# Setup of a fused four-layer kernel: weight loads issued earlier, batch 0 packed ahead of its period, conversions moved to earlier slots

## What is computed

```python
x = L0(x)   # x -> gelu(x down) -> an expert chosen by the batch's id -> up, + x, layer norm
x = L1(x)   # scale and shift from a timestep; attention, 16 heads of 16, with bias and mask; FF of 1024
x = L2(x)   # one of three small MLPs, chosen by the batch's id, + x, layer norm
x = L3(x)   # finite differences of products with five 256x256 grids, x + dt * sum, relu

emb = silu(sin_emb(timestep)) @ W_ada + b_ada      # in L1
q, k, v = x @ Wq + bq, x @ Wk + bk, x @ Wv + bv
probs = softmax(where(mask, -inf, q k' / 4 + attention_bias))
x = x + (probs v) @ Wo + bo
x = x + gelu2(ln(x) * g2 @ W1 + b1) @ W2 + b2
```

## Time and profile before

| | us |
|---|---|
| median of 3 runs | 895.62 (894.95 to 899.71) |
| profiled execution, its own time | 897.77 |
| profiled execution, its span | 896.0 |
| TensorE busy in the span | 817.8 (91%) |
| DVE busy | 739.6 (83%) |
| ACT busy | 623.2 (70%) |

### The profile page before, as it was taken

One profiled execution on the slowest core, in us unless ns is written; L12 is line 12 of the kernel. 1 busy time (PEld: TensorE's weight loads), 2 busy tenths in 40 slices (PEclk: granted clock), 3 DMA queues, 4 the chain that ended last, 5 costly groups with the idle time before them and its releaser, 6 DMA issues.

```text
span 896.0 us, 18592 instructions
## 1 busy us (share of the span) xinstructions
PE 817.8 (91%) x5968; PEld 698.8 (78%) x5968; DVE 739.6 (83%) x2474; ACT 623.2 (70%) x1284; POOL 163.8 (18%) x160
## 2 busy tenths in 40 slices
PE   5576869899999999999999999999999999998692
PEld 2355658788988888888888888888888888787581
DVE  5452787898998989898989899898989898969555
ACT  3153758687878787887878787878788787777230
POOL 3010101222030302122222213030212212201200
PEclk9677989999999999999999999999999999999986
DMA  6356978577585868676676857595758678581110
GB/s 173 117 129 159 206 173 195 129 173 178 133 192 149 190 153 173 156 187 164 157 185 168 189 134 179 151 193 154 183 156 177 162 155 175 138 200 43 53 36 12
DMA packets 147593, 137.33 MB, mean 153 GB/s; under 512 B 19282, under 2 KB 144787, under 8 KB 147492
## 3 DMA queue, kind: packets, MB, share of 16 engines
q1 hardware_dynamic: 147172, 135.80, 63.8%
q10 hardware_dynamic: 320, 0.26, 0.1%
HBM read 98.23 MB, written 4.23 MB: 114 GB/s over the span
## 4 chain that ended last, share of the span: by engine, by line
PE 82%; DVE 9%; issue 3%; SPq 2%; DMA 2%; ACT 1%; POOL 0%; POOLq 0%; DVEq 0%; ACTq 0%
PE back_bank L1109 12%; PE turn_bank L1065 11%; PE score_bank L1184 6%; PE context_bank L1119 6%; PE score_bank L1185 6%; PE front_bank L1103 5%; PE back_bank L1103 5%; PE attend_bank L1103 5%; PE front_bank L1136 3%; PE back_bank L1089 3%; PE front_bank L1290 3%; PE back_bank L1080 3%; PE attend_bank L1089 3%; PE attend_bank L1050 2%; PE front_bank L1338 2%
## 5 line engine op out<-in xcount | busy, mean ns | idle before, releaser
L548 ACT ACTIVATE sc<-sc,negmax 128x256 f32<-128x256 f32 x512 | 231.2, 504 | 20.6 <-DVE negmax L905 20.1
L905 DVE CUSTOM_DVE_ANT_0 sc<-score_bank,side 128x256 f32<-128x256 f32 x512 | 195.3, 419 | 40.4 <-PE score_bank L1185 33.0
L526 ACT ACTIVATE pt<-turn_bank 128x512 f32<-128x512 f32 x176 | 105.9, 602 | 133.3 <-PE turn_bank L1065 112.3
L1065 PE MATMUL turn_bank<-ident,sc 128*128 128x128 f32 x1024 | 158.4, 278 | 1.4 <-ACT sc L548 1.4
L1065 PEld LDWEIGHTS turn_bank<-ident,sc 128*128 128x128 f32 x1024 | 124.3, 142 | 32.6 <-issue 14.1
L1184 PE MATMUL score_bank<-ks,qs 128*128 128x256 f32 x512 | 124.0, 324 | 8.5 <-DVE negmax L905 6.2
L1109 PE MATMUL back_bank<-w,ffT 128*128 128x256 f32 x512 | 118.0, 379 | 0.0
L1109 PEld LDWEIGHTS back_bank<-w,ffT 128*128 128x128 f32 x512 | 97.0, 190 | 12.6
L1185 PE MATMUL score_bank<-mask_neg,ident_r 128*128 128x512 f32 x256 | 102.8, 402 | 0.0
L468 POOL TENSOR_TENSOR rstd<-var,half_neg 128x2 f32<-128x2 f32 x64 | 50.0, 781 | 286.9 <-DVE var L830 285.3
L1184 PEld LDWEIGHTS score_bank<-ks,qs 128*128 128x128 f32 x512 | 79.6, 195 | 16.6 <-issue 7.9
(11 more groups left out here) (216 smaller groups left out, 1978.1 us busy)
## 6 DMA issues: line engine op xcount, KB each, us to landing
side<-in_side SPq DMA_DIRECT2D x128, 512.0 KB, 5.4
qs<-qh SPq DMA_DIRECT2D x128, 64.0 KB, 4.3
qs<-ql SPq DMA_DIRECT2D x128, 64.0 KB, 4.6
wb<-in_wb SPq DMA_DIRECT2D x16, 512.0 KB, 7.2
ks<-kh SPq DMA_DIRECT2D x126, 64.0 KB, 4.1
ks<-kl SPq DMA_DIRECT2D x126, 64.0 KB, 4.5
xN<-in_x SPq DMA_DIRECT2D x16, 256.0 KB, 4.8
wc<-in_wc SPq DMA_DIRECT2D x16, 256.0 KB, 3.1
```

The source lines that it names most:

```text
L526: e.activation(pt[:, h % NP2, :, :], two(tbank[h % 2]), ACT.Copy).then_inc(copied[h % 4], 1)
L548: i = e.activation(sc[:, h % NS, q, :], sc[:, h % NS, q, :], ACT.Exp, bias=negmax[:, q, h:h + 1], scale=-1.0)
L905: i = e.tensor_tensor_reduce(sc[:, s % NS, q, :], two(sbank[s % 2])[:, q, :], side[:, (H * X.i + s) % NSIDE, q, :], -1.0, 3.4e38, ALU.add, ...
L1065: i = e.transpose(tbank[h % 2][:, k * S + q * P:k * S + q * P + P], sc[:, h % NS, q, k * P:k * P + P], ident[:, :])
```

## The change

The load of `w1` takes the place of that of `w2` behind the first inputs; that of `w_ada` goes to a buffer of its own (in `sc`), since `w1` now lies in `ffT`. The rest of the weights, 12 transfers of 3.8 MB in all by their sizes in the code, is issued at turn -1, slot 1. Both halves of batch 0 are packed in turn -1, and period 0 has no `stack(X, B, 1, ..)`. ACT's Gelu table is loaded at the start, and Sin stands behind the first Gelu. The conversions move as in the list.

```diff
             load(ld_bo, (bo[:, :], d["bo"].partition_broadcast(P)), (wo[:, :, :], blocks(d["wo"])))
-            load(ld_bo, (w2[:, :, :], blocks(d["w2"])))
+            load(ld_w1, (w1_raw, blocks(d["w1"])))
...
-            later = {
-                (0, 1): lambda: load(ld_w1, (w1_raw, blocks(d["w1"]))),
-                (0, 3): lambda: load(ld_grid, (t_a[:, :, :], tall(d["grid_B"][0]))),
...
-            }
+            def load_rest():
+                load(ld_bo, (w2[:, :, :], blocks(d["w2"])))
+                load(ld_grid, (t_a[:, :, :], tall(d["grid_B"][0])), (t_b[:, :, :], tall(d["grid_B"][1])), (t_c[:, :, :], tall(d["grid_B"][2])),
+                     (x2[:, :, :], tall(d["grid_A"][0])), (x3[:, :, :], tall(d["grid_A"][1])))
+                load(ld_late, (wa[:, :, :], blocks(d["wa"])), (t_u[:, :, :], blocks(d["d1T"])), (t_r2[:, :, :], blocks(d["d2T"])),
+                     (b2r[:, :], d["b2"].partition_broadcast(P)), (gamma3[:, :], d["gamma3"].partition_broadcast(P)),
+                     (beta3[:, :], d["beta3"].partition_broadcast(P)))
...
+                    if is_step(t, s, -1, 1):
+                        load_rest()
...
-                    if s in (0, 1, 2, 3) and X:
+                    if s in (0, 1, 2, 3) and X and t > 0:
                         stack(X, B, 1, (s,))
...
-                        for b in range(NBLK) if s == 8 else (2, 3):
-                            for u in range(2):
-                                (pack_q, pack_k)[s - 8](e, 0, b, u)
+                        for m, blocks_ in ((0, range(NBLK)),) if s == 8 else ((0, (1, 3)), (1, range(NBLK))):
+                            for b in blocks_:
+                                for u in range(2):
+                                    (pack_q, pack_k)[s - 8](e, m, b, u)
+                                    if m == 1:
+                                        pack_q(e, m, b, u)
...
+            e.wait_ge(pool_set, IDENT_SET)
+            e.activation(first_switch[:, :], ident[:, 0:1], ACT.Gelu)
...
-                    if t == 1 and s in (1, 2):
+                    if is_step(t, s, -1, 8):
                         e.wait_ge(ld_w1, 16)
-                        e.activation(w1[:, s - 1, :], w1_raw[:, s - 1, :], ACT.Copy, scale=g2c[:, s - 1:s]).then_inc(act_set, 1)
-                    if is_step(t, s, 1, 5):
+                        for k in range(KT):
+                            e.activation(w1[:, k, :], w1_raw[:, k, :], ACT.Copy, scale=g2c[:, k:k + 1]).then_inc(act_set, 1)
+                    if is_step(t, s, -1, 11):
                         e.wait_ge(ld_bo, 3 * 16)
                         e.activation(w2[:, :, :], w2[:, :, :], ACT.Copy, scale=0.5).then_inc(act_set, 1)
...
-                    for t0, s0, setup in ((-2, 5, set_high), (-2, 14, set_low_q), (-1, 2, set_first_ada), (-1, 3, set_rest), (-1, 4, set_ada_rows),
-                                          (-1, 7, set_value_bias), (-1, 11, set_output_bias), (1, 1, set_first_bias), (1, 2, set_scaled_grids),
-                                          (1, 3, set_first_low), (1, 4, set_more_grids), (1, 5, set_sum_grids), (1, 7, set_edges),
-                                          (2, 1, set_conditional), (2, 3, set_derivatives)):
+                    for t0, s0, setup in ((-2, 14, set_high_q), (-1, 2, set_first_ada), (-1, 3, set_low_q), (-1, 6, set_rest), (-1, 6, set_ada_rows),
+                                          (-1, 7, set_value_bias), (-1, 9, set_first_low), (-1, 10, set_output_bias), (-1, 11, set_scaled_grids),
+                                          (-1, 12, set_more_grids), (0, 1, set_sum_grids), (0, 3, set_conditional), (0, 5, set_edges),
+                                          (0, 7, set_derivatives), (0, 11, set_first_bias)):
```

More of the change, by code:

```diff
@@ L333, in _ @@
                  (upT[0:A, :], d["upT"]), (upT[ONE:ONE + 1, :], d["up_b"].rearrange("(a n) -> a n", a=1)))
-            load(ld_ada_w, (ffT[:, 0:4, :], blocks(d["w_ada"])))
+            load(ld_ada_w, (w_ada, blocks(d["w_ada"])))
             e.wait_ge(dve_set, IDS_SET)
@@ L594, in body @@
                         i.then_inc(ev["kh_ready"], 1)
+                        if t == -1:
+                            e.wait_ge(ev["kh_ready"], F.n)
+                            e.wait_ge(pool_set, KS_SET)
+                            for b in (0, 2):
+                                for u in range(2):
+                                    pack_k(e, 0, b, u)
                     if s == 9 and F:
@@ L717, in in_halves, with set_high @@
                 return w[:, k, m * P:m * P + P].rearrange("p (u d h) -> p u d h", d=DH, u=2)
[L719 to L724, removed]
+            def set_high(raw, high, low, scale):
+                for k, m, u in parts:
+                    i = e.tensor_scalar(in_halves(high, k, m)[:, u, :, :], by_half(raw, k, m)[:, u, :, :], scale, None, ALU.mult)
+                link(i)
             def set_low(raw, high, low, scale):
@@ L730, in set_low, with set_high_q @@
                 link(i)
-            def set_low_q():
-                set_low(*raws[0])
+            def set_high_q():
+                e.wait_ge(ld_proj, 3 * 16)
+                set_high(*raws[0])
             def set_first_ada():
@@ L738, in set_first_ada, with set_low_q, set_rest @@
                 link(e.tensor_copy(ada[:, 1, :], abank[:, D:2 * D]))
+            def set_low_q():
+                link(e.tensor_scalar(bq, bq, DH ** -0.5, None, ALU.mult))
+                set_low(*raws[0])
+                e.sem_inc(dve_set, 1)
+            def set_rest():
+                set_high(*raws[1])
+                link(e.tensor_copy(wv[:, :, :], th[:, 0, :, :]))
                 set_low(*raws[1])
[L741 to L744, removed]
+                link(e.tensor_tensor(wvl[:, :, :], th[:, 0, :, :], wv[:, :, :].bitcast(F32), ALU.subtract))
                 e.sem_inc(dve_set, 1)
@@ L1150, in body @@
                                 cond = x1late[:, k, 0:1].broadcast_to([P, P]) if rows == P else x1late[:, k, 0:NB]
-                                e.matmul(dst, cond, ffT[:, 2 * k:2 * k + 2, :], start=(k == 0), stop=False)
+                                e.matmul(dst, cond, w_ada[:, k, :], start=(k == 0), stop=False)
                             i = e.matmul(dst, ones_row[:, 0:rows], b_ada, start=False, stop=True)
```

39 lines of the change are left out of this document (12 added, 27 removed).

## The result

| | median us | all executions |
|---|---|---|
| before | 895.29 | 894.2 to 899.71 (4) |
| changed | 883.36 | 882.13 to 884.87 (4) |

The ratio is 0.9858, with a 95% interval of 0.982 to 0.9896: 11.9 us less. 881.5 was predicted, with a range of 876 to 889. The profiled execution took 884.87 us, its span 883.1, against 897.77 before. The total is thus near, but it is made of parts that were not all right, and these are what the profile shows.

The account below looks back on a forecast made before the run. TensorE was taken as the bound from 198 us on, so only its idle time before that could move. Terms -0.5 - 1.4 - 1.5 - 8.5 - 2.3 = -14.2 us led to 881.5 us, range 876 to 889.

Parts of the forecast that it names:

- Lead-in (A): Work up to the first scores of layer 0: about 0.5 us earlier, first scores at 50.4.
- w2 term of 1.1: In the lead-in, ACT's scaling of w2 between the two g delays the second g and first scores by 1.1 us.
- the prediction's own sign of 40: Store of ada_rows before the first packs: landing after 40 us would show the queue forecast wrong; 38.4 was expected.
- the second rival: Early weight loads run slower than 365 GB/s, at 217; first scores 6.2 us late, end 887.6; chance 0.17.
- Period 0 (B): Up to qh of batch 1: the 7.3 us pack wait goes, setup fills most of it; -1.4 us beside A.
- the sum 66.65 - 0.5 + 7.0 - 1.0 = 72.1: Forecast time of qh of batch 1: old end of q, lead-in gain, setup added, less short waits of DVE.
- Head 0 of batch 1 (C): Before the first scores of batch 1: one grid load less and a faster last pack landing; -1.5 us.
- the 0.6 of the grid load: Before head 0 of batch 1, SP has one grid load less to issue: 0.6 us gained.
- the predicted -3.4 to the first scores of batch 1: First scores of batch 1 come 3.4 us earlier in all.
- Period 1 (D): DVE's setup leaves period 1, where PE waited for DVE, and PE's clock rises: -8.5 us.
- Period 2 (E): set_conditional leaves period 2 and with it PE's idle time of 2.3 us: -2.3 us.
- The third rival: Setup in period 0 hides in waits for scores, qh near 67 to 68; another -4.5, end 877; chance 0.13.

Follow-up runs that it names:

- e7: Changed kernel plus 16 unused 512-column matmuls, 8 each in slots 3 and 5 of period 0: 880.93 us.
- e5: Changed kernel with ACT's scaling of w2 moved behind the second g of layer 0 instead of between the two: 882.03 us.
- the repetition: The changed kernel measured once more, unaltered, beside later runs on the same chip: 884.60 us.
- e1: Changed kernel with four setup steps (sum_grids, edges, conditional, derivatives) put back from period 0 to their old places in periods 1 and 2: 886.15 us.
- e3: Changed kernel's loads and packs, with all conversions it had moved out of periods 1 and 2 put back there: 890.41 us.
- e4: Changed kernel with conditional, derivatives, sum_grids and edges moved from period 0 into DVE's gaps of the lead-in: 876.29 us.
- e9: Changed kernel with sum_grids, conditional, edges and derivatives moved from slots 1, 3, 5 and 7 of period 0 to its slot 9: 877.00 us.
- e6: Changed kernel with the store of the conditional vectors issued by ACT instead of by SP behind the twelve loads: 883.01 us.
- e11: Changed kernel with the four setup steps in slot 9, w2 scaling behind the second g, store on ACT's queue, plus 16 unused matmuls: 874.67 us.

## Why the prediction was right, and where its terms were wrong

**Lead-in (A), predicted -0.5, measured +0.1.** The expert's matmul came 0.7 earlier and not 0.9 (12.56 after 13.29). The moves of DVE were as forecast: `n3l` 2.3 earlier (28.42), `ql` 2.1 earlier (33.36). Then the term lacked the clock: k's twelve matmuls took 2.89 us at 0.50 instead of 1.72 at full clock. That is no fixed price of the change, since k took 1.96 in e7 with the same lead-in, and the kernel before has one profile only. The w2 term of 1.1 was right (0.9 in e5).

**The packs.** The store landed at 39.4 and not 38.4, the packs began at 39.8, and the first half was issued by 47.5. Its last pack landed at 49.5, as written: 1.5 us ahead of the first scores here, 0.7 ahead in the repetition, where the store landed at 40.2, past the prediction's own sign of 40. In three profiles with a quicker lead-in the packs came last, and the first scores waited for them: 0.65 us in e7, 2.0 in e1, 2.4 in e3. Moving 3.8 MB ahead of a small transfer delayed it from 1.6 to 6.1, the behaviour the prediction reckoned with; the loads ran at 363 GB/s at 34 to 36 us, so the second rival's 217 GB/s did not come.

**Period 0 (B), predicted -1.4, measured +0.8 beside A.** The prediction set its forecast against 73.98, the second of the two writes of `qh`. Against the first, 73.61, its 72.1 is -1.5 in all and -1.0 beside A, and the 7.3 us of waiting are 7.0. The step that failed is the sum 66.65 - 0.5 + 7.0 - 1.0 = 72.1. It prices DVE's setup and leaves PE's own work at its old length. The price of the setup was nearly right: from the first scores to the start of q it is now 20.52 us instead of 14.03, +6.5 against the +6.0 of the sum, and +6.1 in the repetition. Then q takes 2.93 instead of 1.69: 1.2 us that the text had no term for. With the 0.6 of A that makes the 2.4 between 72.1 and 74.50. Ahead of q PE waited for DVE's steps (2.69, 2.53 and 2.00 us), with the clock at 0.50 from 52 to 62 us where it had been 0.66. That the steps are the reason for the half clock is likely but not shown, as e5, e1 and e3 say above.

**Head 0 of batch 1 (C), predicted -1.5, measured -1.0**, counted from 73.61 and 74.50. The landing fell from 5.95 to 5.0, as written, and is all of it: from `qh` to the issue of the pack it is 23.07 us before and after, so the 0.6 of the grid load that is gone did not come. Gains and losses offset each other there: up to the one-column matmuls of the first bias 7.99 us instead of 8.70, in them 4.71 instead of 3.73, behind them 10.37 instead of 10.64. In the 4.71 us PE's clock was 1.00 at the start and fell to 0.50 at about 84.8, while PE was busy without a gap. Of the predicted -3.4 to the first scores of batch 1, -0.06 came; in the repetition, where these scores started at 101.69, -1.0.

**Period 1 (D), predicted -8.5, measured -8.5** from the first scores of batch 1 to those of batch 2 (50.15 to 41.66), by the means named: the wait for `n` is down to 1.3, the clock is 1.00. e3 shows the cause, as putting the conversions back brings the wait of 4.1 back; those of DVE and of ACT were not put back one by one. **Period 2 (E), -2.3, measured -3.2** between the xa steps; e1 has it back, with 51.9.

So the total was right because D held, and in part by luck: E and the remainder behind 186 us (1.1, for which the prediction had no term and which no run explains) gave 2 us more, while A, B and C gave 3.3 less. The third rival (setup hides in period 0, 877) was not what this order does, but it named the price: at places where it does hide, e4 and e9 measured 876.3 and 877.0.

What stays open: why the same code ran q at full clock in e5 and at half in the changed kernel, and at half in e1 and at full in e9, and how much of the 1.3 to 2.6 us of e5 is that.

## What to carry to other kernels

When a stall is removed by filling it with moved work, ask where each engine stands idle, not which period does: 7.8 us of setup cost 7 to 8 us in slots 1 to 7 and nothing in slot 9 of the same period. A move that makes TensorE wait in short pieces can have a second price, since its next matmuls may run at half clock; count their work at both clocks (q: 1.7 and 2.9 us), and don't read a difference of that size from one profile. And big early loads ahead of a small transfer on which a queue stands still should be summed up to that transfer's landing, with the margin named: here it was 1.5 us in one profile, 0.7 in the next of the same kernel, and gone in three others. The 28 packs in one row had a price too, since the small load of the expert's weight stood behind them and held DVE for up to 3.9 us once the setup was out of its way.

## What was not expected of the hardware

- SP's issue of two 256 KB loads took 4.01 us (22.25) behind three `side` loads and a 1 MB load, where the next one took 0.56. The other twelve profiles with these loads have 3.6 to 4.5 us there. What held the issue no run here took apart.
- Sixteen matmuls that nobody needs made the kernel about 2 us faster (880.93 against the 883.01 of e6), and the granted clock of 62 to 75 us was 1.00 with them, 0.72 in e6 and 0.65 in the changed kernel. In e11, where the clock was 1.00 without them, they gained nothing.
- A 32 KB store on a queue of its own, with the DMA engines full of another queue's loads, landed after 4.8 us, not 1.6, but ahead of the last of those loads.
- The same code ran at either clock: q of batch 1 took 2.92 us in e1 and 1.70 in e9, which do not differ up to there.
